# A graph-attention layer on one core: the last 512 adjacency columns of the last quarter summed densely, and the tail of the program put in another order

## The chip, the cores and the metric

One core of a Trainium2 chip. The metric is the device time of one execution in microseconds (us); of several executions the median counts. All arrays start and end in HBM.

## The reference

The input is x, 4096 nodes of 128 features in float32, and a 4096x4096 adjacency of zeros and ones, denser towards low row and column numbers (an entry is 1 with a probability that falls as one over the root of both numbers). What is computed, cut short:

```python
h = relu(layernorm(x))
Wh = h @ W0
e = leaky_relu((Wh @ a[:128])[:, None] + (Wh @ a[128:])[None, :], 0.2)
e = where((adj > 0) | eye(N), e, -9e15)
x = x + softmax(e, axis=1) @ Wh
h = relu(layernorm(x))
weights = where(adj < 1.0, exp(-(1/adj - 1)**2 / 0.5), 0.0)
return x + weights @ (h @ W1 + B)
```

For an adjacency of zeros and ones the last sum is zero, so the program checks that no entry is anything else and would take a general path (not run here) if one were.

## The kernel before, in words

The 64 MB of the adjacency are read once, as 32 chunks of 2 MB (128 partitions x 4096 numbers) through a ring of six buffers, `adj_ring`. `chunk(i)` (line 58) says what chunk i holds: quarter s of the rows (1024 rows each), column block c (1024 columns), and half h (512 of the quarter's rows). Two chunks with the same s and c make a step; there are four steps to a quarter, sixteen in all. In the last quarter the column blocks come in the order 3, 0, 1, 2 (steps 12 to 15, chunks 24 to 31).

Each chunk is read by three engines.

- TensorE packs it (`pack`, L613 to L645): for every 512 columns one matmul writes a code of the column (L629), and four matmuls per half chunk add the entries times powers of two (L642), so that after both halves of a step a PSUM bank holds, per partition and column, one word with the bits of eight rows.
- VectorE or ScalarE checks that its entries are zeros and ones: VectorE for 13 chunks in one SCALAR_TENSOR_TENSOR (L1134), 26 and 28 among them, ScalarE for 19 in two passes (L952, L961), 24, 25, 27, 29, 30 and 31 among them.
- A buffer is given back when it is packed and checked; SyncE then issues the load of the chunk six later (L394 to L405).

From the words the edges are found. VectorE takes the eight largest words of each stretch of columns (`scan`, L1162, MAX8 into `cand`), then picks the best per partition over the steps of a piece (`pick`, L1175; `PIECES`, line 75, says which steps make a piece: steps 0 to 3, 4 to 7, 8 to 11, 12 to 14, and 15 alone). What a partition picks beyond its own slots goes into slots that a set of partitions shares (`place` on TensorE, L683; `pick_shared`, L1208; `place_shared`, L710). `decode` (L1295) and `decode_shared` (L1252) turn words into a column number and row bits. GpSimd then fetches a row of `node_table` (130 numbers of a node: its weight factor and scaled features) per slot by indirect DMA (L544), in groups g of eight such gathers or fewer. VectorE makes edge weights and spreads them (`weigh`, L1321), and TensorE adds them to eight accumulator tiles by matmuls (`scatter`, L773, sixteen matmul records for eight tiles). The last group, g = 9, has four gathers, each weighed and added by itself (`weigh_last`, L1380; `scatter_last`, L790). Group 6 (eight gathers) and 7 (eight shared gathers) belong to the third quarter, group 8 to steps 12 to 14, group 9 to step 15.

Beside this run dense parts for the first 128 columns (`column`, L1422; `add_columns`, L740) and for each node's edge to itself (`own_weights`, L979, on ScalarE; `add_own`, L758). When all groups of a quarter are added, `epilogue(s)` (L1445) divides and adds x; the last quarter's is split in three (`finish_last`, L1462), each with its own store.

There is no scheduler: each engine runs its instructions in the order of the code. The tables of lines 122 to 145 say behind which chunk i of its main loop an engine does what (SCAN_AT, PICK_AT, DECODE_AT, WEIGH_AT, CHECK_LATE, EPILOGUE_AT on VectorE, SCATTER_AT, PLACE_BEHIND, ADD_COLUMNS_AT and ADD_OWN_AT on TensorE), and lines 602 to 616 (VectorE) and 849 to 859 (TensorE) are the tail behind the loop. Engines wait for one another by semaphores.

## Time and profile before

| what | value |
|---|---|
| median of 3 runs | 216.37 us (216.04 to 217.75) |
| the profiled execution | 217.44 us |
| its span, first to last instruction | 215.6 us |
| busy in the span: TensorE, VectorE, ScalarE, GpSimd | 72%, 84%, 88%, 62% |
| read from HBM | 74.06 MB |

The span is the stretch that the profile covers; the execution's own time has 1.84 us more around it. The profiled execution is slower than the median by 1.07 us, so that differences are worked out inside the profile and laid on the median. In the rows below, times are us from the span's start.

### The profile page before, as it was taken

How to read it: one execution, taken by the hardware profiler on the slowest of the kernel's cores; microseconds unless marked ns; L12 is line 12 of the kernel's file. 1: busy time of each engine (PE TensorE's matmuls, PEld its weight loads, DVE VectorE, ACT ScalarE, POOL GpSimd, SP SyncE). 2: the span in 40 equal slices, each digit the busy share in tenths (PEclk: the TensorE clock that was granted, in tenths of full speed). 3: DMA queues.
4: the chain of work that ended last, by engine and by line, in shares of the span. 5: the costliest groups of instructions: out<-in, count | busy, mean ns of one | idle time of the engine just before them, and what ended most of it. 6: DMA issues, size and time to landing. Idle time of an engine off the chain costs nothing.

```text
span 215.6 us, 3229 instructions
## 1 busy us (share of the span) xinstructions
PE 154.3 (72%) x956; PEld 103.7 (48%) x970; DVE 182.0 (84%) x535; ACT 189.3 (88%) x207; POOL 132.8 (62%) x140
## 2 busy tenths in 40 slices
PE   0186779983794992989929997499392977799472
PEld 0074565440362760549615844186341654668361
DVE  7993999999979999999488796995986499878855
ACT  0699987599899999999999999799999994999960
POOL 3980002295000588888878888888787788667450
PEclk9999999996599698599985999999979799999995
DMA  5999999999999999999999999999999999961303
GB/s 166 355 413 410 410 408 408 409 411 405 418 418 409 409 393 405 391 400 393 402 388 387 394 401 394 404 387 400 394 387 389 386 401 393 406 229 43 115 23 103
DMA packets 22259, 76.81 MB, mean 356 GB/s; under 512 B 2527, under 2 KB 3126, under 8 KB 22240
## 3 DMA queue, kind: packets, MB, share of 16 engines
q1 hardware_dynamic: 18912, 71.31, 84.7%
q0 software_dynamic: 2912, 5.22, 7.0%
q8 instruction: 8, 0.13, 0.2%
q10 hardware_dynamic: 416, 0.07, 0.2%
q14 instruction: 11, 0.09, 0.1%
HBM read 74.06 MB, written 4.23 MB: 363 GB/s over the span
## 4 chain that ended last, share of the span: by engine, by line
DMA 36%; DVE 31%; PE 18%; issue 7%; ACT 5%; SPq 1%; POOL 1%; POOLq 0%; DVEq 0%
DMA adj_ring<-in_adj 35%; DVE summed L1134 10%; PE bank L642 9%; DVE cand L1172 3%; ACT spread L921 3%; DVE hub_w L1415 3%; PE bank L769 2%; DVE x_sb L1458 2%; PE bank L754 2%; PE bank L761 2%; SPq L383 1%; DMA gathered_rows<-node_table,shared_index 1%; DVE stats L1114 1%; PE bank L629 1%; DVE shared_slots L1230 1%
## 5 line engine op out<-in xcount | busy, mean ns | idle before, releaser
L544 POOL DMA_INDIRECT gathered_rows<-node_table,index x48 | 76.0, 1584 | 36.5 <-DVE index L1309 22.5
L952 ACT ACTIVATE trash_a<-adj_ring,below_one 128x4096 fp8e4<-128x4096 f32 x19 | 70.4, 3705 | 5.7 <-DMA adj_ring<-in_adj 5.2
L642 PE MATMUL bank<-adj_ring,pack_w 128*128 128x512 bf16 (+3 forms) x255 | 70.0, 402 | 2.4 <-DMA adj_ring<-in_adj 1.5
L961 ACT ACTIVATE trash_a<-adj_ring 128x4096 fp8e4<-128x4096 f32 x19 | 68.7, 3614 | 0.5
L1134 DVE SCALAR_TENSOR_TENSOR summed<-adj_ring 128x4096 fp8e4<-128x4096 f32 x13 | 58.0, 4458 | 4.3 <-DMA adj_ring<-in_adj 4.2
L642 PEld LDWEIGHTS bank<-adj_ring,pack_w 128*128 128x128 bf16 x262 | 26.1, 104 | 31.5 <-issue 8.8
L544 POOL DMA_INDIRECT gathered_rows<-node_table,shared_index x24 | 33.2, 1382 | 9.6 <-issue 6.7
L1172 DVE MAX8 cand<-bank 128x8 f32<-128x120 f32 (+25 forms) x82 | 23.3, 351 | 3.9 <-PE bank L642 3.9
L769 PE MATMUL bank<-gathered_rows,spread 128*128 128x129 f32 x160 | 20.9, 282 | 3.9 <-DVE spread L1398 2.4
L769 PEld LDWEIGHTS bank<-gathered_rows,spread 128*128 128x128 f32 x160 | 19.4, 194 | 5.1 <-issue 4.8
L629 PE MATMUL bank<-codes,code_w 128*128 128x512 bf16 x25 | 11.2, 448 | 8.5 <-DMA adj_ring<-in_adj 5.6
L678 PE MATMUL bank<-whe,hub_w 128*128 128x129 f32 x64 | 10.4, 316 | 5.1 <-DVE hub_w L1419 5.0
L921 ACT ACTIVATE spread<-x_sb,shift,rstd 128x128 f32<-128x128 f32 x32 | 13.2, 497 | 0.3 <-DVE shift L1126 0.3
L678 PEld LDWEIGHTS bank<-whe,hub_w 128*128 128x128 f32 x64 | 9.1, 219 | 7.0 <-DVE hub_w L1419 6.8
L491 POOL PARTITION_ALL_REDUCE ends_all<-ends x1 | 1.4, 1442 | 17.3 <-DVE ends L1539 17.3
L565 PE MATMUL bank<-ident,spread 128*128 128x128 f32 x32 | 6.3, 327 | 7.8 <-ACT spread L921 7.8
L577 PE MATMUL bank<-w_sb,gathered_rows 128*128 128x130 f32 x64 | 9.8, 300 | 1.4 <-ACT whe L935 1.3
L1442 DVE SCALAR_TENSOR_TENSOR col_w<-r_rows,hub_whe,bank 128x512 f32<-128x512 f32 (+1 forms) x6 | 4.2, 708 | 7.4 <-PE bank L609 7.4
L629 PEld LDWEIGHTS bank<-codes,code_w 128*128 128x128 bf16 x32 | 3.7, 115 | 13.7 <-DMA adj_ring<-in_adj 6.2
L577 PEld LDWEIGHTS bank<-w_sb,gathered_rows 128*128 128x128 f32 x64 | 8.6, 208 | 2.7 <-ACT gathered_rows L927 2.4
L985 ACT ACTIVATE own_w<-ident,w_self 128x128 f32<-128x128 f32 x32 | 9.7, 386 | 0.0
L699 PE MATMUL bank<-slots,own_lane 128*32 128x16 f32 (+1 forms) x24 | 1.4, 188 | 10.5 <-issue 10.5
(190 smaller groups left out, 258.4 us busy)
## 6 DMA issues: line engine op xcount, KB each, us to landing
adj_ring<-in_adj SPq DMA_DIRECT2D x32, 2048.0 KB, 23.6
node_table<-gathered_rows POOLq DMA_DIRECT2D x4, 520.0 KB, 8.3
x_sb<-in_x SPq DMA_DIRECT2D x8, 256.0 KB, 5.9
out<-x_sb SPq DMA_DIRECT2D x3, 512.0 KB, 14.2
gathered_rows<-node_table,index POOLq DMA_INDIRECT x48, 5.9
gathered_rows<-node_table,shared_index POOLq DMA_INDIRECT x24, 5.4
out<-x_sb SPq DMA_DIRECT2D x2, 192.0 KB, 2.1
out<-x_sb SPq DMA_DIRECT2D x1, 128.0 KB, 1.9
```

The costliest lines, as they stand in the source:

```text
L544: pool.indirect_dma_start(out=rows[:, g % RING_GROUPS * GE + t, :], out_offset=None, in_=table, in_offset=bass.IndirectOffsetOnAxis(ap=row ...
L577: last = nc.tensor.matmul(bank[6 + half][:, b * (D + 2):(b + 1) * (D + 2)], hT[:, nb * P:(nb + 1) * P], w0_sb[:, :], start=(b == 0), stop= ...
L629: nc.tensor.matmul(to[:, :], code_w[:, 2 * c + half, :], codes[:, :], start=True, stop=False, skip_group_check=True)
L642: last = nc.tensor.matmul(to[:, lo:hi], pack_w[:, k, :], ring_hi[:, i % AR, row_at + lo:row_at + hi], start=False, stop=(k == KB - 1), ski ...
L678: last = nc.tensor.matmul(bank[7][:, 0:E1], hub_w[:, m % 2, b, :], whe[:, 4 * HUB_ORDER[m] + b, ONE:ONE + E1], start=(m + b == 0), stop=(m ...
L769: return nc.tensor.matmul(acc_of(SUPER_OF_GROUP[g], t), spread[:, g % 2, at * KB:(at + 1) * KB, :], rows[:, g % RING_GROUPS * GE + turn, G ...
L921: last = nc.scalar.activation(hn_block(b), x_sb[:, b, :], ACT.Identity, bias=shift[:, b:b + 1], scale=rstd[:, b:b + 1])
L952: nc.scalar.activation(trash_a[:, :], ring[:, i % AR, :], ACT.Sign, bias=below_one[:, :], scale=-1.0, accum_out=signs[:, n:n + 1], saturat ...
L961: nc.scalar.activation(trash_a[:, :], ring[:, i % AR, :], ACT.Abs, accum_out=sizes[:, n:n + 1], saturate=False).then_inc(checked_a, 1)
L985: last = nc.scalar.activation(own_w[:, t, :], ident[:, :], ACT.Copy, scale=w_self[:, nb:nb + 1])
L1134: nc.vector.scalar_tensor_tensor(trash_v, ring[:, i % AR, :], 1.0, ring[:, i % AR, :], ALU.is_ge, ALU.not_equal, accum_out=bad_v[:, n:n + ...
L1172: last = nc.vector.max(cand[:, at * 8:(at + 1) * 8], word_bank(step, half)[:, lo:hi])
```

## The change

The last chunk of the adjacency is no longer a half of step 15. `kernel()` on the host lays the last quarter's columns 2048 to 3071 out anew, without arithmetic, as an input `adj_tail` of two times 2 MB beside the old one. Its first half holds columns 2048 to 2559 for all 1024 rows in the packing's layout. This is chunk 28, the narrow one; it makes step 14 alone, in one PSUM bank. Step 15 is column block 1, whose halves are chunks 29 and 30. The second half of `adj_tail`, chunk 31, holds columns 2560 to 3071 turned, so that partitions are columns, in four blocks of 128 columns, each with its own DMA and semaphore. These are not packed and scanned: VectorE multiplies each block with the weights max(row factor, column factor) (`weigh_dense`, one SCALAR_TENSOR_TENSOR of 128x1024), and TensorE adds it to the eight accumulator tiles (`add_dense`). The 512 rows of the node table for that are loaded by SyncE ahead of chunk 20 into `summed`, in which the checks of VectorE wrote until chunk 11; from chunk 14 on they write over `hub_mask`.

The third quarter's shared slots get sets of eight partitions rather than four (`PIECES`), so that its group 7 has four gathers in place of eight; for that a second table of row factors (`r_oct2`) is made near the start. The tables that order the loop are changed from chunk 25 on, and the tail behind the loop is written anew.

```diff
+NARROW, DENSE = 28, CHUNKS - 1
+DENSE_AT = 5 * BW
+DB = 4
 def chunk(i):
+    if i >= NARROW:
+        return SG - 1, 1 if i in (29, 30) else 2, int(i > 29)
...
-PIECES = [((0, 1, 2, 3), 32, 16, 32, 4), ((4, 5, 6, 7), 24, 16, 16, 4), ((8, 9, 10, 11), 24, 8, 32, 4),
+PIECES = [((0, 1, 2, 3), 32, 16, 32, 4), ((4, 5, 6, 7), 24, 16, 16, 4), ((8, 9, 10, 11), 24, 8, 32, 8),
...
-CHECK_LATE = {22: 22, 27: 26, 29: 28}
+CHECK_LATE = {22: 22, 26: 26, 30: 28}
...
-ADD_COLUMNS_AT = {13: 0, 21: 1, 28: 2}
-EPILOGUE_AT = {20: 0, 28: 1}
...
+ADD_COLUMNS_AT = {13: 0, 21: 1, 27: 2}
+EPILOGUE_AT = {20: 0, 27: 1, 31: 2}
...
+                if i == NARROW:
+                    sp.dma_start(ring[:, i % AR, :].rearrange("p (a n) -> p a n", a=HK),
+                                 adj_tail[0].rearrange("a p n -> p a n")).then_inc(adj_ready[i % AR], 16)
+                    return
+                if i == DENSE:
+                    for b in range(DB):
+                        sp.dma_start(dense_adj[:, b, :], adj_tail[1, b]).then_inc(dense_ready[b], 16)
+                    return
...
+                if i == 20:
+                    sp.wait_ge(table_stored, 16 * SG)
+                    sp.wait_ge(checked_v, DVE_CHECKED.index(14))
+                    sp.dma_start(dense_whe, table[DENSE_AT:DENSE_AT + BW, :].rearrange("(p b) c -> p b c", b=DB)).then_inc(
+                        dense_whe_loaded, 16)
...
+            def add_dense(b):
+                pe.wait_ge(dense_set, b + 1)
+                pe.wait_ge(dense_whe_loaded, 16)
+                for t in range(KB):
+                    nc.tensor.matmul(acc_of(SG - 1, t), dense_w[:, b, t, :], dense_whe[:, b, GQ:GQ + E1], start=False,
+                                     stop=True, skip_group_check=True)
...
+            def weigh_dense(b):
+                dve.wait_ge(dense_ready[b], 16)
...
+                nc.vector.scalar_tensor_tensor(dense_w[:, b, :, :].rearrange("p t m -> p (t m)"),
+                                               r_rows[:, :, :].rearrange("p t m -> p (t m)"), dense_whe[:, b, AQ:AQ + 1],
+                                               dense_adj[:, b, :], ALU.max, ALU.mult).then_inc(dense_set, 1)
...
-            weigh(7)
             scan(STEPS - 1)
             pick(4)
-            epilogue(2)
+            weigh_dense(0)
             pick_shared(4)
+            weigh_dense(1)
             decode_shared(4)
+            weigh_dense(2)
             weigh(8)
+            weigh_dense(3)
             weigh_last(0)
```

The first place is VectorE around the check of chunk 26 (the SCALAR_TENSOR_TENSOR of 128x4096), at the start of the last quarter. `cand<-bank2` are the scans of step 13, `edge_w` begins `weigh(6)`, `rden` begins `epilogue(1)`. Before:

```order
L1372 TENSOR_TENSOR spread<-same,hq_of_e 128x512
L1442 SCALAR_TENSOR_TENSOR col_w<-r_rows,hub_whe,bank7 128x8x64 [waits col_turned,col_added,r_rows_set]
L1134 SCALAR_TENSOR_TENSOR summed,bad<-adj_ring 128x4096 [waits checked_v,adj_ready2]
L1442 SCALAR_TENSOR_TENSOR col_w<-r_rows,hub_whe,bank7 128x8x64 [waits col_turned]
L1172 MAX cand<-bank2 128x8 [waits packed]
...
L1348 TENSOR_TENSOR edge_w<-r_slots,gathered_rows 128x64 [waits spread_set,gathered2,bits_set]
...
L1453 RECIPROCAL rden<-bank4 128x3 [waits acc_read,scattered]
...
L1134 SCALAR_TENSOR_TENSOR summed,bad<-adj_ring 128x4096 [waits checked_v,adj_ready4]
L1172 MAX cand<-bank0 128x8 [waits packed]
```

Now; L1204 is the check, L1543 the column weights, L1554 the epilogue:

```order
L1473 TENSOR_TENSOR spread<-same,hq_of_e 128x512
L1204 SCALAR_TENSOR_TENSOR hub_mask,bad<-adj_ring 128x4096 [waits checked_v,adj_ready2]
L1543 SCALAR_TENSOR_TENSOR col_w<-r_rows,hub_whe,bank7 128x8x64 [waits col_turned,col_added,r_rows_set]
L1554 RECIPROCAL rden<-bank4 128x3 [waits acc_read,scattered]
...
L1440 TENSOR_TENSOR edge_w<-r_slots,gathered_rows 128x64 [waits spread_set,gathered2,bits_set]
...
L1543 SCALAR_TENSOR_TENSOR col_w<-r_rows,hub_whe,bank7 128x8x64 [waits col_turned]
L1242 MAX cand<-bank2 128x8 [waits packed]
...
L1440 TENSOR_TENSOR same<-r_oct2,gathered_rows 128x256 [waits spread_set,gathered3,shared_on_set]
...
L1242 MAX cand<-bank0 128x8 [waits packed]
```

The check of chunk 26 now stands ahead of both column weights, and the epilogue ahead of `weigh(6)`; `weigh(7)` (`same<-r_oct2`), which came behind step 14 and its decoding, now stands ahead of step 14's scan (`cand<-bank0`), with the check of chunk 28 behind that.

The second place is the tail of VectorE: `pick_shared(4)` begins with `placed<-bank7`, `decode_shared(4)` with `shared_i<-bank7` and gives `shared_index`, for which GpSimd waits with group 9. Before:

```order
L1185 TENSOR_REDUCE fullest<-cand 128x1 [waits placed_set,full_seen,merged,scanned]
...
L1453 RECIPROCAL rden<-bank4 128x3 [waits acc_read,scattered]
...
L1458 SCALAR_TENSOR_TENSOR x_sb<-bank4,rden,x_sb 128x128 [waits epilogue_step]
...
L1221 TENSOR_TENSOR placed<-bank7,iota 16x64 [waits shared_placed_set,shared_seen,shared_picked,merged]
...
L1266 CAST shared_i<-bank7 128x4 [waits shared_on_set,shared_index_set,shared_done]
...
L1278 TENSOR_TENSOR shared_index<-shared_column,shared_empty 128x4 [waits weight_step,gathered1,shared_step]
...
L1348 TENSOR_TENSOR edge_w<-r_slots,gathered_rows 128x64 [waits spread_set,gathered0,bits_set]
...
L1387 SCALAR_TENSOR_TENSOR same<-r_oct,gathered_rows,shared_on 128x64 [waits spread_set,shared_on_set,last_gathered0]
```

Now; L1403 is `weigh_dense`:

```order
L1554 RECIPROCAL rden<-bank4 128x3 [waits acc_read,scattered]
...
L1242 MAX cand<-bank2 128x8 [waits picked,packed]
...
L1255 TENSOR_REDUCE fullest<-cand 128x1 [waits placed_set,full_seen,merged,scanned]
...
L1403 SCALAR_TENSOR_TENSOR adj_ring<-r_rows,summed,adj_ring 128x1024 [waits col_turned,packed,checked_v,dense_whe_loaded,dense_ready0]
L1296 TENSOR_TENSOR placed<-bank7,iota 16x64 [waits shared_placed_set,shared_seen,shared_picked,merged]
...
L1403 SCALAR_TENSOR_TENSOR adj_ring<-r_rows,summed,adj_ring 128x1024 [waits dense_ready1]
L1341 CAST shared_i<-bank7 128x4 [waits shared_on_set,shared_index_set,shared_done]
...
L1353 TENSOR_TENSOR shared_index<-shared_column,shared_empty 128x4 [waits weight_step,gathered1,shared_step]
...
L1403 SCALAR_TENSOR_TENSOR adj_ring<-r_rows,summed,adj_ring 128x1024 [waits dense_ready2]
L1440 TENSOR_TENSOR edge_w<-r_slots,gathered_rows 128x64 [waits spread_set,gathered0,bits_set]
...
L1403 SCALAR_TENSOR_TENSOR adj_ring<-r_rows,summed,adj_ring 128x1024 [waits dense_ready3]
L1488 SCALAR_TENSOR_TENSOR same<-r_oct,gathered_rows,shared_on 128x64 [waits spread_set,shared_on_set,last_gathered0]
```

`epilogue(2)` (`rden<-bank4`) has gone from behind the last pick to ahead of the last scan (`cand<-bank2`), and four `weigh_dense` stand in the tail, two of them ahead of `shared_index`.

The third place is the tail of TensorE, from the last shared words on. Before (L761 is `add_own`, L769 the scatter):

```order
L719 MATMUL bank7<-turn_of_tq,stats 128x4 [waits shared_placed_set]
L761 MATMUL bank0<-whe,own_w 128x129 [waits own_w_set]
L761 MATMUL bank0<-whe,own_w 128x129 x2
...
L769 MATMUL bank0<-gathered_rows,spread 128x129 [waits spread_set,gathered0]
...
L769 MATMUL bank0<-gathered_rows,spread 128x129 [waits part_spread,last_gathered0]
...
L769 MATMUL bank0<-gathered_rows,spread 128x129 [waits part_spread,last_gathered1]
```

Now (L797 is `add_dense`, L831 the scatter):

```order
L797 MATMUL bank0<-summed,adj_ring 128x129 [waits dense_whe_loaded,dense_set]
...
L777 MATMUL bank7<-turn_of_tq,stats 128x4 [waits shared_placed_set]
L797 MATMUL bank0<-summed,adj_ring 128x129 [waits dense_whe_loaded,dense_set]
...
L797 MATMUL bank0<-summed,adj_ring 128x129 [waits dense_whe_loaded,dense_set]
...
L831 MATMUL bank0<-gathered_rows,spread 128x129 [waits spread_set,gathered0]
...
L797 MATMUL bank0<-summed,adj_ring 128x129 [waits dense_whe_loaded,dense_set]
...
L831 MATMUL bank0<-gathered_rows,spread 128x129 [waits part_spread,last_gathered0]
...
L831 MATMUL bank0<-gathered_rows,spread 128x129 [waits part_spread,last_gathered1]
```

`add_own` has gone ahead of this place, and four times eight dense products of float32 stand around the last words and the last whole group, one of them between that group and the four parts of the last one.

## Rows read from the trace of the kernel before

**Rows 1.** The page's slices of the span, 40 equal ones: DMA busy in tenths.
```profile
DMA  5999999999999999999999999999999999961303
```
**Rows 2.** Timeline of TensorE: start us, us, line, operation, operands, count, idle time before and releaser.
```profile
165.46 0.39 PE L629 MATMUL bank<-codes,code_w 128*128 128x512 bf16 x1 [4.03 <-DMA adj_ring<-in_adj]
...
177.00 0.39 PE L629 MATMUL bank<-codes,code_w 128*128 128x512 bf16 x1 [1.35 <-DMA adj_ring<-in_adj]
...
204.94 2.47 PE L769 MATMUL bank<-gathered_rows,spread 128*128 128x129 f32 x20 [1.20 <-DVE spread L1359]
...
209.50 0.68 PE L769 MATMUL bank<-gathered_rows,spread 128*128 128x129 f32 x4 [0.68 <-DVE spread L1398]
211.21 1.20 PE L769 MATMUL bank<-gathered_rows,spread 128*128 128x129 f32 x4 [1.03 <-DVE spread L1398]
```
**Rows 3.** Timeline of VectorE, the last quarter up to the last scan.
```profile
169.84 0.75 DVE L1442 SCALAR_TENSOR_TENSOR col_w<-r_rows,hub_whe,bank 128x512 f32<-128x512 f32 x1 [4.35 <-PE bank L609]
170.51 4.42 DVE L1134 SCALAR_TENSOR_TENSOR summed<-adj_ring 128x4096 fp8e4<-128x4096 f32 x1
...
178.42 0.30 DVE L1453 RECIPROCAL rden<-bank 128x3 f32<-128x3 f32 x3
...
180.70 4.42 DVE L1134 SCALAR_TENSOR_TENSOR summed<-adj_ring 128x4096 fp8e4<-128x4096 f32 x1
...
185.04 1.49 DVE L1172 MAX8 cand<-bank 128x8 f32<-128x24 f32 x5
...
190.98 0.43 DVE L1348 TENSOR_TENSOR same<-r_quad,gathered_rows 128x256 f32<-128x256 f32 x1 [0.41 <-DMA gathered_rows<-node_table,shared_index]
...
194.59 1.43 DVE L1172 MAX8 cand<-bank 128x8 f32<-128x272 f32 x4 [1.47 <-PE bank L642]
```
**Rows 4.** Timeline of VectorE, the tail behind the last pick.
```profile
196.48 0.30 DVE L1453 RECIPROCAL rden<-bank 128x3 f32<-128x3 f32 x3
...
198.76 0.20 DVE L1221 TENSOR_TENSOR placed<-bank,iota 16x64 f32<-16x64 f32 x1
...
201.79 0.16 DVE L1266 CAST shared_i<-bank 128x4 int32<-128x4 f32 x1 [0.41 <-PE bank L719]
...
202.19 0.16 DVE L1278 TENSOR_TENSOR shared_index<-shared_column,shared_empty 128x4 int32<-128x4 int32 x1
...
203.05 0.22 DVE L1348 TENSOR_TENSOR edge_w<-r_slots,gathered_rows 128x64 f32<-128x64 f32 x1
...
203.56 1.22 DVE L1359 TENSOR_TENSOR spread<-edge_w,lane_of_p 128x1024 f32<-128x1024 f32 x1
...
209.27 0.17 DVE L1468 RECIPROCAL rden<-bank 128x3 f32<-128x3 f32 x1
...
210.26 0.28 DVE L1387 SCALAR_TENSOR_TENSOR same<-r_oct,gathered_rows,shared_on 128x64 f32<-128x64 f32 x1
...
212.66 0.61 DVE L1472 SCALAR_TENSOR_TENSOR x_sb<-bank,rden,x_sb 128x128 f32<-128x128 f32 x2
```
**Rows 5.** Timeline of GpSimd: gathers of groups 6 and 7.
```profile
166.08 1.00 POOL L544 DMA_INDIRECT gathered_rows<-node_table,index  x1 [0.30 <-issue]
167.38 1.00 POOL L544 DMA_INDIRECT gathered_rows<-node_table,shared_index  x1 [0.30 <-issue]
...
171.29 4.50 POOL L544 DMA_INDIRECT gathered_rows<-node_table,shared_index  x1 [0.30 <-issue]
...
180.98 5.01 POOL L544 DMA_INDIRECT gathered_rows<-node_table,shared_index  x1 [0.30 <-issue]
```
**Rows 6.** The page's DMA issues: operands, engine, count, median us from issue to landing.
```profile
gathered_rows<-node_table,shared_index POOLq DMA_INDIRECT x24, 5.4
```
**Rows 7.** Stretches: us; busy us of PE, PEld, DVE, ACT, POOL; TensorE clock granted; DMA share; GB/s.
```profile
111.50:118.20 6.70, 5.69 (x29) 3.44 (x30) 5.88 (x22) 6.67 (x7) 5.18 (x6) 0.50 1.03 385
...
166.10:169.40 3.30, 3.30 (x10) 1.23 (x9) 0.00 (x0) 3.27 (x3) 2.69 (x3) 0.50 1.03 394
...
210.50:213.50 3.00, 1.43 (x6) 1.01 (x6) 2.37 (x12) 0.00 (x0) 0.00 (x0) 0.50 0.36 130
```

More of the change, by code:

```diff
@@ L106, in piece_segments @@
     s = SUPER_OF_PIECE[n]
-    columns = {chunk(2 * step)[1] for step in PIECES[n][0]}
-    return [x for x in SEGMENTS[s] if x[0] // 2 in columns]
+    banks = {b for step in PIECES[n][0] for b in banks_of(step)}
+    return [x for x in SEGMENTS[s] if x[0] in banks]
 NCAND = max(len(piece_segments(n)) for n in range(len(PIECES))) * 8
@@ L611, in turn_columns, with pack_narrow @@
                 last.then_inc(col_turned, 1)
+            def pack_narrow():
+                pe.wait_ge(adj_ready[NARROW % AR], (NARROW // AR + 1) * 16)
+                step = step_of(NARROW)
+                to = word_bank(step, 0)
+                pe.wait_ge(scanned, scanned_by(step - 2) - 1)
+                nc.tensor.matmul(to[:, :], code_w[:, banks_of(step)[0], :], codes[:, :], start=True, stop=False,
+                                 skip_group_check=True)
+                for k in range(KB):
+                    last = nc.tensor.matmul(to[:, :], pack_w[:, k, :], ring_hi[:, NARROW % AR, k * BW:(k + 1) * BW],
+                                            start=False, stop=(k == KB - 1), skip_group_check=True)
+                last.then_inc(packed, 1)
             def pack(i):
+                if i == NARROW:
+                    return pack_narrow()
                 s, c, h = chunk(i)
-                step = i // 2
+                step = step_of(i)
                 pe.wait_ge(adj_ready[i % AR], (i // AR + 1) * 16)
@@ L816, in _ @@
             lane_scores()
-            for i in range(CHUNKS):
+            for i in range(DENSE):
                 pack(i)
@@ L948, in check @@
                 n = ACT_CHECKED.index(i)
-                act.wait_ge(adj_ready[i % AR], (i // AR + 1) * 16)
+                if i == DENSE:
+                    for b in range(DB):
+                        act.wait_ge(dense_ready[b], 16)
+                else:
+                    act.wait_ge(adj_ready[i % AR], (i // AR + 1) * 16)
                 if n >= 1:
```

208 lines of the change are left out of this document (130 added, 78 removed).

## The prediction

> **What bounds the kernel now.** I read the page's slices first: the DMA engines are nine tenths busy or more from the second slice through the 35th [rows 1], so the chunks arrive as fast as they can until the slice that begins at 188.7 us, and then there is a tail of some 23 us in which little is loaded. Next the timelines, to see what that tail consists of. TensorE waits for chunk 26 at 165.46 and for chunk 28 at 177.00 [rows 2], that is 5.8 us a chunk; the last scan starts at 194.59, released by TensorE's packing of chunk 31 [rows 3]. From there one chain runs to the end: last scan and pick, `epilogue(2)`, the shared pick (198.76), the shared decoding with `shared_index` at 202.19, the last gathers, their weights, and the last division, which ends at 212.66 + 0.61 = 213.27 [rows 4]. The stores make the rest of the 215.6 us.
>
> But VectorE, not chunk 31, sets the pace before that. From the column weights at 169.84 on it has short waits only, 0.41 for a gather and 1.47 for the last packing [rows 3], and before that one long one, 4.35, for the first columns of the quarter. The reader should keep three things apart: VectorE's own work, the gathers that it waits for, and the last chunk. The change shortens what depends on the last chunk and adds work to VectorE and TensorE.
>
> **Up to group 7: what the moved check fills, and what it holds up.** The load of 512 table rows ahead of chunk 20 (128 x 520 numbers, 266 KB) goes through the saturated SyncE queue. At the 394 GB/s of a late stretch [rows 7] that is 0.7 us on every later chunk. Its bounds are 0, if the four removed gathers give that time back, and 0.7; I take 0.6 and have chunk 26 at 166.1. The check of chunk 26, 4.42 us [rows 3], now runs there at once, to 170.5, in the hole of 4.35 us. Taken alone that gains all of it.
>
> The hole was covered by nothing on VectorE, but GpSimd was gathering in it. The gather that began at 171.29, 0.78 us into the check of 170.51, took 4.50 us instead of 1.00 and ended at 175.79, which is 0.86 behind the check's end at 174.93; the one at 180.98 did the same beside the check of 180.70 [rows 3, 5]. So a check costs GpSimd one gather of its own length. Now it meets the last gather of group 6, which began at 166.08 [rows 5]: this ends at 170.5 + 0.9 = 171.4. The four gathers of group 7 follow at GpSimd's pitch of 1.3 (166.08 to 167.38), at 171.7, 173.0, 174.3 and 175.6, and the last lands 5.4 later [rows 6], at 181.0. VectorE gets there earlier: column weights to 171.3, `epilogue(1)` 2.28 (178.42 to 180.70) to 173.6, group 6 landing at 166.08 + 5.4 + 4.4 = 175.9, its weights 1.73 (as 203.05 to 204.78 [rows 4]), columns 0.75 and a scan of 1.49 to 179.9. `weigh(7)` thus waits for 1.1 us and starts at 181.0. From issue to landing a gather is bounded below by its issue, 1.00, and above by 6.0: the one held from 180.98 to 185.99 was what VectorE waited for until 190.98, 10.0 later, 4.0 of them its hold. I take the median of the page, which is near the upper end.
>
> At this place the trace and a rule part. The Trainium skill (SBUF — State Buffer, Who interferes with whom) infers that a VectorE operation with two SBUF inputs takes only the read side of the port that it shares with GpSimd, and that writing descriptors needs the other side, so that such an operation would not hold up a gather. The gather of 4.50 us beside a two-input check says that it does here. By the rule the stall would go; what that gives is the first rival.
>
> **From group 7 to the last index.** `weigh(7)` takes 2.14 (190.98 to 194.59 - 1.47 = 193.12 [rows 3]), to 183.1. From the scan of step 14 to the end of the shared pick of piece 3 was 185.04 to 190.98 - 0.41 = 190.57, 5.53 us; the narrow step has two maxima in place of five, 3/5 of 1.49 less: 4.6, to 187.7. The check of chunk 28 takes 4.34 (180.70 to 185.04), to 192.1; `epilogue(2)` 2.28 (196.48 to 198.76 [rows 4]), to 194.4. The last scan and pick take 1.89 (194.59 to 196.48), to 196.3. So VectorE is done here at 196.3 with what in before it had done at 198.76: 2.5 us ahead. TensorE has chunk 30 packed by then: at 5.8 us a chunk it lands by 189.2, and TensorE's work behind the merge of the third piece (chunk 29, group 7, six column tiles, chunk 30) is some 7 us from 185.8, to 193.
>
> `weigh_dense` has no row. Nearest are the same operation on 512 elements, 0.75, and on 4096, 4.42 [rows 3]; between them lie 1.02 ns an element, so 1024 take 1.27, of which about 0.07 overlaps with the next, as with the columns (0.75 against a start to start of 0.67, 169.84 to 170.51). I take 1.2; the bounds stay 0.75 and 4.42. Two of them stand ahead of the index: 196.3 + 1.2 = 197.5; the shared pick 2.62 (198.76 to 201.79 - 0.41 = 201.38), 200.1; the second, 201.3; decoding to the index 0.56 (201.79 to 202.19 + 0.16), 201.9 against 202.35. Of the 2.5 us ahead, 2.4 are two dense blocks less 0.4 of waiting that they cover: 0.45 remain. Chunk 31, at the same 5.8 us a chunk, is there by 195, before its first block is used, and is no longer waited for.
>
> **The end.** Decoding ends 1.26 behind its start, at 202.6; the third block 203.8; `weigh(8)` 1.73, 205.5; the fourth block 206.7. On TensorE 16 matmuls of float32 take 2.47 - 0.68 = 1.79 us (20 against 4 [rows 2]). From 203.8 it has the third block, group 8, the fourth block and two parts of the last group: 16 + 16 + 16 + 8 matmuls, 6.3 us with nothing between, 210.2 with 0.1 to start. TensorE, which waited here in before, now ends last. The last gathers, 0.45 earlier and perhaps 0.9 later for a `weigh_dense` beside them, land by 210.3 and are covered. Then as in before: the first division 0.99 (209.27 to 210.26), 211.2; the last weights 0.95 (210.26 to 211.21), 212.15; four matmuls 0.68 at full clock in place of 1.20, 212.85; last division 0.86 (212.41 to 213.27), 213.7. That is 0.4 later than 213.27. The profiled execution of 217.44 would be 217.9, and on the median 216.37 + 0.4 = **216.8 us**. A measurement tells about 1% (2.2 us) from no change, so this is no change.
>
> The other edits I cost at nothing. The second `r_oct` table and its matmul fall near the start, where the chunks come as fast as the DMA engines allow; without that cover they are under 1 us. Four blocks and a narrow chunk are the same bytes in the same rows of 4 KB. `own_weights(3)` now runs while ScalarE waits for chunk 29, so ScalarE ends some 2 us earlier, but nobody waits for it.
>
> **Rivals.** (1) The gathers are not held up. Then group 7 lands at 171.29 + 5.4 = 176.7, before VectorE comes to it (171.3 + 2.28 + 1.73 + 0.75 + 1.49 = 177.5), and all behind it moves up by 181.0 - 177.5 = 3.5, TensorE's packing of chunk 28 (177.6, 2.0 us) just allowing it: 216.8 - 3.5 = **213.3, faster**. This is what the skill's rule on the shared port would make of it. Against it are both held gathers of rows 5; for it, that 166.08 and 166.1 are a tie: should that one gather pass ahead, 1.3 us are won (215.5, still no change). (2) TensorE's clock falls in the dense blocks. It was at its lower level, 1.2 GHz, from 166.1 to 169.4 behind 4.03 us without work, for 6.7 us from 111.5, and from 210.5 on, where the same four matmuls took 1.20 in place of 0.68 [rows 2, 7]. The blocks come with gaps between them from 196 on. If it falls at the place where TensorE ends last, after 203.8, a stretch of 3.3 to 6.7 us does half the work and costs 1.7 to 3.3: 218.5 to 220.1, **219.3, slower**. It decides only there; earlier, VectorE covers it. Against it: between 203.8 and 210 TensorE would have no gap at all. (3) The change does not do what it says, because group 8 is gathered late: its eight gathers start near 187, the check of chunk 28 holds one for 4 us, and GpSimd may come to the last group only at 202.4. That is 0.5 us, 217.3, inside no change.
>
> **How the numbers follow.** Forecast, with (3) and the tie: 0.59. Rival (1) and other ways in which waits vanish: 0.24. Rival (2) and dense weights nearer their upper bound (each 1 us more on three of them is 3 us): 0.17. So faster by over 1% 0.24, within 1% 0.59, slower 0.17. The forecast's own range is 215.3 (0.75 a block, three of them on the path, -1.4) to 218.4 (gather latency, +1, and a short fall of the clock). For 8 in 10 it must reach into both rivals: 213.0 to 219.6.
>
> **What would show it.** Right: a check of 4.4 us from about 166, one gather beside it that ends 0.9 behind it, `weigh(7)` waiting for a gather at about 181, `weigh_dense` at 1.2, TensorE without a gap from 204 to 210, the last division ending near 213.7. Wrong: `weigh(7)` before 179, or TensorE's clock at half behind 200, or a scan of step 15 that waits for TensorE.

## The result, and the profile after

The changed kernel takes 219.17 us in the median (219.11 to 219.82) where the kernel before takes 216.53 beside it (216.04 to 217.75): a ratio of 1.0123, 95% interval 1.0091 to 1.0155. It is slower by a little more than 1%. It lies inside the range of 213.0 to 219.6, near its upper end, and above the forecast's own 215.3 to 218.4: the forecast of 216.8 and of "no change" was 2.4 us too low. A second set of runs of the same kernel gave 220.14 (218.98 to 220.60), ratio 1.0152 (1.0114 to 1.0191). Ratios are of undisturbed runs of the same set, without those over 1.5% above a kernel's fastest (below: two of ten without dense work, its profiled one among them, five of ten without dense work but with filler, five of twelve with the orders combined), so they can differ from the quotient of two medians.

The profiled execution took 219.82 us, span 218.0, last division at 215.12 + 0.61 = 215.73 (213.27 before, forecast 213.7). VectorE's timeline, the last quarter up to the last scan, which answers to [rows 3]:

```profile
166.24 4.41 DVE L1204 SCALAR_TENSOR_TENSOR hub_mask<-adj_ring 128x4096 fp8e4<-128x4096 f32 x1
...
176.03 0.23 DVE L1440 TENSOR_TENSOR edge_w<-r_slots,gathered_rows 128x64 f32<-128x64 f32 x1 [2.43 <-issue]
...
181.30 0.42 DVE L1440 TENSOR_TENSOR same<-r_oct,gathered_rows 128x256 f32<-128x256 f32 x1 [1.59 <-issue]
...
186.40 0.17 DVE L1377 CAST words_i<-bank 128x8 int32<-128x8 f32 x1 [0.79 <-PE bank L764]
...
188.33 4.43 DVE L1204 SCALAR_TENSOR_TENSOR hub_mask<-adj_ring 128x4096 fp8e4<-128x4096 f32 x1
...
195.69 1.49 DVE L1242 MAX8 cand<-bank 128x8 f32<-128x24 f32 x5 [0.64 <-PE bank L700]
```

The check of chunk 26 stands where it was forecast, and the two waits for gathers are there, 2.43 and 1.59 (forecast 2.3 and 1.1). The profile names no releaser for them; each ends 4.5 to 4.6 us behind the end of the last gather that the group needs (171.52 and 176.72 on GpSimd), and from 164 us on a gather of this run takes 2.5 to 5.5 us from issue to landing. New is the last line: the last scan waits 0.64 us for TensorE's packing of chunk 30, and ahead of the decoding at 186.40 VectorE waited 0.79 for TensorE, where before it was 0.55 for the same step. The reason stands in TensorE's timeline, beside [rows 2]:

```profile
165.88 0.39 PE L687 MATMUL bank<-codes,code_w 128*128 128x512 bf16 x1 [1.83 <-DMA adj_ring<-in_adj]
...
185.26 0.57 PE L757 MATMUL bank<-slots,own_oct 128*16 128x8 f32 x16 [3.89 <-issue]
...
186.59 1.92 PE L700 MATMUL bank<-adj_ring,pack_w 128*128 128x512 bf16 x4
...
193.69 1.97 PE L700 MATMUL bank<-adj_ring,pack_w 128*128 128x512 bf16 x8
...
211.12 1.50 PE L831 MATMUL bank<-gathered_rows,spread 128*128 128x129 f32 x12
214.16 0.68 PE L831 MATMUL bank<-gathered_rows,spread 128*128 128x129 f32 x4 [1.54 <-DVE spread L1499]
```

TensorE stood 3.89 us ahead of the placing of piece 3 (L757). The four packing matmuls at 186.59 then take 1.92 us; in the run with filler below, at full clock, four take 1.06. Two stretches give the granted clock as the last but two figure (columns as in [rows 7]):

```profile
185.26:189.50 4.24, 4.10 (x25) 2.06 (x27) 3.25 (x14) 4.21 (x4) 1.58 (x2) 0.50 1.03 414
203.00:212.50 9.50, 8.90 (x76) 8.64 (x76) 7.71 (x26) 3.55 (x3) 4.17 (x4) 1.00 0.08 16
```

So TensorE's clock was at its lower level (1.2 GHz) from 185.3 to 189.5, and at the full one (2.4 GHz) behind 203, where the second rival had looked for its fall. The tail on VectorE, beside [rows 4]:

```profile
198.08 1.28 DVE L1403 SCALAR_TENSOR_TENSOR adj_ring<-r_rows,summed,adj_ring 128x1024 f32<-128x1024 f32 x1 [0.34 <-issue]
...
203.41 0.17 DVE L1353 TENSOR_TENSOR shared_index<-shared_column,shared_empty 128x4 int32<-128x4 int32 x1
...
208.37 0.32 DVE L1488 SCALAR_TENSOR_TENSOR same<-r_oct,gathered_rows,shared_on 128x64 f32<-128x64 f32 x1
...
212.21 0.18 DVE L1569 RECIPROCAL rden<-bank 128x3 f32<-128x3 f32 x1 [1.55 <-PE bank L831]
...
213.22 0.27 DVE L1488 SCALAR_TENSOR_TENSOR same<-r_oct,gathered_rows,shared_on 128x64 f32<-128x64 f32 x1
...
215.12 0.61 DVE L1573 SCALAR_TENSOR_TENSOR x_sb<-bank,rden,x_sb 128x128 f32<-128x128 f32 x2
```

A dense block takes 1.28 us (1.20 from start to start). No weighing of group 8 or 9 waits for a gather any more: `weigh(8)` at 205.53 and `weigh_last(0)` at 208.37 follow their predecessors. VectorE works without a pause from 198.08 to 210.66 and then waits 1.55 us for TensorE. The index is 1.2 later than before (203.58 against 202.35 at its end), and from there to the last division's end it is 12.15 us against 10.92.

GpSimd, beside [rows 5]: the gather that met the check ends 0.87 us behind it (166.24 + 4.41 = 170.65), and the four of group 7 follow. Later the check of chunk 28 holds the second gather of group 8 in the same way (4.65 us from 189.00).

```profile
166.89 4.63 POOL L588 DMA_INDIRECT gathered_rows<-node_table,index  x1 [0.30 <-issue]
171.82 1.00 POOL L588 DMA_INDIRECT gathered_rows<-node_table,shared_index  x1 [0.30 <-issue]
```

### The profile page after: what moved, and what is told of

The parts are those of the page before. It is cut to its first block, busy times and chain, and to the rows that moved or that the text cites. A ratio compares the mean times of both kernels' runs of the same rounds, so it can differ in the third digit from the quotient of the medians.

```text
span 218.0 us, 3371 instructions
## 1 busy us (share of the span) xinstructions
PE 160.5 (74%) x1021; PEld 111.0 (51%) x1035; DVE 186.8 (86%) x539; ACT 190.0 (87%) x209; POOL 124.2 (57%) x136
## 4 chain that ended last, share of the span: by engine, by line
DVE 30%; PE 26%; DMA 22%; issue 10%; ACT 9%; SPq 1%; DVEq 0%
DMA adj_ring<-in_adj 22%; PE bank L700 8%; DVE summed L1204 8%; PE bank L831 4%; DVE hub_w L1516 3%; DVE cand L1242 3%; ACT spread L987 3%; PE bank L814 3%; PE bank L822 2%; PE bank L797 2%; ACT trash_a L1022 2%; ACT trash_a L1031 2%; PE bank L687 1%; DVE adj_ring L1403 1%; SPq L447 1%
## 5 line engine op out<-in xcount | busy, mean ns | idle before, releaser
L588 POOL DMA_INDIRECT gathered_rows<-node_table,index x48 | 76.8, 1599 | 44.3 <-DVE index L1384 30.8
L700 PE MATMUL bank<-adj_ring,pack_w 128*128 128x512 bf16 (+3 forms) x239 | 67.5, 409 | 3.7 <-DMA adj_ring<-in_adj 2.5
L700 PEld LDWEIGHTS bank<-adj_ring,pack_w 128*128 128x128 bf16 x246 | 25.1, 106 | 31.5 <-issue 10.1
L1204 DVE SCALAR_TENSOR_TENSOR summed<-adj_ring 128x4096 fp8e4<-128x4096 f32 x7 | 31.5, 4500 | 0.1
L1204 DVE SCALAR_TENSOR_TENSOR hub_mask<-adj_ring 128x4096 fp8e4<-128x4096 f32 x6 | 26.5, 4419 | 4.8 <-DMA adj_ring<-in_adj 4.8
L588 POOL DMA_INDIRECT gathered_rows<-node_table,shared_index x20 | 23.8, 1192 | 8.6 <-issue 5.8
L1242 DVE MAX8 cand<-bank 128x8 f32<-128x120 f32 (+25 forms) x80 | 22.7, 350 | 3.1 <-PE bank L700 3.1
L831 PE MATMUL bank<-gathered_rows,spread 128*128 128x129 f32 x160 | 20.0, 277 | 1.5 <-DVE spread L1499 1.5
L831 PEld LDWEIGHTS bank<-gathered_rows,spread 128*128 128x128 f32 x160 | 19.3, 193 | 2.2 <-issue 2.0
L797 PE MATMUL bank<-summed,adj_ring 128*128 128x129 f32 x64 | 8.1, 280 | 1.5 <-DVE adj_ring L1403 1.5
L1516 DVE TENSOR_SCALAR hub_w<-r_hub,whe 128x128 f32<-128x128 f32 x32 | 8.9, 354 | 0.0
```

The lines of the kernel that those rows point to most:

```text
L588: pool.indirect_dma_start(out=rows[:, g % RING_GROUPS * GE + t, :], out_offset=None, in_=table, in_offset=bass.IndirectOffsetOnAxis(ap=row ...
L700: last = nc.tensor.matmul(to[:, lo:hi], pack_w[:, k, :], ring_hi[:, i % AR, row_at + lo:row_at + hi], start=False, stop=(k == KB - 1), ski ...
L831: return nc.tensor.matmul(acc_of(SUPER_OF_GROUP[g], t), spread[:, g % 2, at * KB:(at + 1) * KB, :], rows[:, g % RING_GROUPS * GE + turn, G ...
L1204: nc.vector.scalar_tensor_tensor(trash_v[int(i >= 14)], ring[:, i % AR, :], 1.0, ring[:, i % AR, :], ALU.is_ge, ALU.not_equal, accum_out=b ...
L1242: last = nc.vector.max(cand[:, at * 8:(at + 1) * 8], word_bank(step, half)[:, lo:hi])
L1516: last = nc.vector.tensor_scalar(hub_w[:, m % 2, b, :], r_hub[:, :], whe[:, nb, QA:QA + 1], whe[:, nb, AA:AA + 1], ALU.mult, ALU.max)
```

## The experiments

Whole times of one kernel differ by 1.6 us and more from run to run, and the check of chunk 26 begins anywhere from 165.6 to 167.0 with the loads. What a step does is therefore also read in the profiled execution, as the stretch from the start of that check to the start of the last division, called the late stretch here. It is one execution of each kernel, and the two of the changed kernel differ by 0.64 us, so smaller differences can be chance.

| run | ratio to before (95%) | late stretch, us |
|---|---|---|
| changed kernel | 1.0123 (1.0091 to 1.0155) | 48.88 |
| the same again | 1.0152 (1.0114 to 1.0191) | 48.24 |
| chunk 29 packed first | 1.0116 (1.0074 to 1.0158) | 47.95 |
| filler ahead of the placing | 1.0119 (1.0079 to 1.0158) | 47.90 |
| no dense sums | 1.0131 (1.0078 to 1.0183) | 49.43 |
| no dense work | 1.0020 (0.9987 to 1.0054) | 46.87 |
| no dense work, with filler | 0.9945 (0.9899 to 0.9991) | 43.61 |
| end reordered | 1.0063 (1.0027 to 1.0099) | 48.13 |
| check of chunk 26 late | 1.0122 (1.0083 to 1.0161) | (moved) |
| orders combined | 0.9961 (0.9925 to 0.9997) | 45.48 |
| and group 6 behind the scan | 0.9906 (0.9875 to 0.9937) | 43.82 |

**TensorE's pause, by order and by filler.** The first:

```
-PLACE_BEHIND = {15: 1, 23: 2, 28: 3}
+PLACE_AT = {8: 0, 29: 3}
+PLACE_BEHIND = {15: 1, 23: 2}
```

> Only the order on TensorE differs from the changed kernel: chunk 29 is packed ahead of the placing of piece 3 instead of behind it. Theory A (the 3.89 us in which TensorE stood before that placing left it at half clock, and the packings of chunks 29 and 30 came late for VectorE's last scan): the first packing matmuls of chunk 29 start near 182.7 us and take 1.07 us each four instead of 1.92, the placing starts where it did, the decode comes 0.2 us sooner, chunk 30 is packed by about 192 us, the last scan follows the epilogue without its 0.64 us wait, and the whole comes out near 218.3 us (0.9 us less than 219.2). Rival B (VectorE covers it, what it gains at the scan it waits again later, for TensorE's dense sums): 219.0 to 219.3 us. In both the last third from the last index to the end stays at 12.1 us.

The second leaves the order alone and adds, ahead of that `place(3)`:

```
+if i == 28:
+    pe.wait_ge(col_w_set, 2 * SG)
+    for _ in range(12):
+        nc.tensor.matmul(bank[7][:, :], pack_w[:, 0, :], ring_hi[:, NARROW % AR, 0:BW], start=True,
+                         stop=True, skip_group_check=True)
```

> The changed kernel's order is kept; twelve packing matmuls of 512 columns whose sums nobody reads are added on TensorE in the 3.89 us in which it stood before the placing of piece 3 (some 2.7 us of work, so about 1.2 us of standing are left). They take no work away, so only the clock can give something back. Theory A (it is the half clock after the pause): the placing's 16 matmuls take 0.3 instead of 0.57 us, the packing of chunk 29 goes at 1.07 us for four, chunk 30 is packed by about 193.3 us instead of 195.7, the last scan does not wait, and the time is near 218.3 us. Rival B (it is the order, chunk 29 behind the placing, and not the clock): the granted clock may rise, but the last scan still waits for TensorE, and the time is within 0.2 us of 219.2.

TensorE's timeline in the run with filler:

```profile
181.45 2.88 PE L910 MATMUL bank<-adj_ring,pack_w 128*128 128x512 bf16 x12
185.48 0.55 PE L757 MATMUL bank<-slots,own_oct 128*16 128x8 f32 x16 [1.16 <-issue]
...
186.42 1.06 PE L700 MATMUL bank<-adj_ring,pack_w 128*128 128x512 bf16 x4
...
191.56 1.97 PE L700 MATMUL bank<-adj_ring,pack_w 128*128 128x512 bf16 x8
```

Its clock in the stretch behind the placing, 1.00 in place of 0.50:

```profile
185.20:189.50 4.30, 4.02 (x38) 2.84 (x39) 3.51 (x15) 4.27 (x4) 1.59 (x2) 1.00 1.02 413
```

VectorE's decoding and its last scan there:

```profile
186.38 0.17 DVE L1382 CAST words_i<-bank 128x8 int32<-128x8 f32 x1 [0.55 <-PE bank L764]
...
194.95 1.48 DVE L1247 MAX8 cand<-bank 128x8 f32<-128x24 f32 x5
```

Added work made TensorE faster: four packing matmuls take 1.06 again, the decoding waits 0.55 instead of 0.79, the last scan not at all, and the late stretch is 0.98 shorter; with the order changed it is 0.93. So the half clock is what delays TensorE, since no order differs here: from the placing to the end of chunk 30's packing it takes 8.05 us (185.48 to 193.53) in place of 10.40 (185.26 to 195.66). The whole time did not follow: both ratios are that of the first set. That is why the changed kernel was run again.

> The changed kernel itself, unaltered, beside the others of this row, because the runs with the placing moved and with filler were shorter by 0.9 us from the check of chunk 26 to the last division (47.9 against 48.9 us) and yet not in their whole time. If the load-bound part ahead of that check varies from run to run and with the place where a kernel runs, this kernel comes out at or above its first 219.2 us here (219.2 to 220.3), with the stretch from that check to the last division again 48.8 to 49.0 us. If instead the 0.9 us are paid back before the check by those two kernels themselves, it is again at 219.2 and its check again begins at 166.2 us where theirs began at 166.5 and 167.0.

The first of the two expectations held for the whole time, 220.14, 0.6 to 0.8 above the two others, though on another chip (the kernel before took 216.59 beside it and 216.44 beside them). It did not hold for the late stretch, 48.24, beside which the filler's is only 0.34 shorter. TensorE's timeline:

```profile
185.70 0.55 PE L757 MATMUL bank<-slots,own_oct 128*16 128x8 f32 x16 [3.90 <-issue]
...
189.15 1.22 PE L700 MATMUL bank<-adj_ring,pack_w 128*128 128x512 bf16 x3
```

VectorE in the same execution:

```profile
195.39 1.48 DVE L1242 MAX8 cand<-bank 128x8 f32<-128x24 f32 x5
```

Again a pause of 3.90 and half clock behind it, but three matmuls from 189.15 take 1.22, and the granted clock is 1.00 from 189.6 on, where in the first execution it is still 0.50 up to 190.5; the packing of chunk 30 just makes it, and the last scan does not wait. Six profiles have this pause, of 3.79 to 4.17 us. In them the last scan waited 0, 0, 0.64, 0.65, 0.77 and 0.77 us for TensorE, and the decoding 0.77 to 0.79 in five and 0.55 in one. The clock costs up to 0.24 at the placing and 0 to 0.8 at the scan. A gain of 0.6 to 0.8 in the whole time is within the intervals, so the ratios do not show it: that the clock delays the last scan is shown, that repairing it shortens the whole is not.

**What the dense columns cost.** All four `weigh_dense` and all four `add_dense` calls are taken out in the first run, the `add_dense` calls alone in the second, so both results lack those columns.

> Leaves out the last 512 columns' work: the four weighings of the dense blocks on VectorE and the four sums on TensorE. Their loads stay. Theory: two weighings (2.5 us) stand before the last index, so it comes at about 201.0 instead of 203.58 us, and behind it nothing of the two other weighings and of TensorE's 64 matmuls is left; the end is then set by the last gathers, issued from 201.9 us on and landed near 208.9, so weigh and scatter of the last part end near 210.2 and the last division near 211.3: about 214.8 us in all, 4.4 less. Rival (the dense work lies beside the gathers, as the weighing of group 8 did in the kernel before): 217.5 us or more.

> Leaves out the four dense sums on TensorE (64 matmuls), keeps the four weighings on VectorE. Theory (TensorE ends last from the third dense sum on): the last index stays at 203.6 us, the first division starts behind the third part's weighing at about 210.7 instead of 212.21 us, without a wait for TensorE, and the whole is near 217.7 us, 1.5 less. Rival (VectorE ends last, TensorE only seems late): within 0.3 us of 219.2. With the run without any dense work this splits the price into VectorE's part and TensorE's.

Both fell short. Without the sums nothing was won at all. TensorE's scatters of that run:

```profile
207.16 5.40 PE L831 MATMUL bank<-gathered_rows,spread 128*128 128x129 f32 x28 [4.91 <-DVE spread L1447]
```

The granted clock in its pause, and in those scatters:

```profile
203.00:207.00 4.00, 0.00 (x0) 0.00 (x0) 3.90 (x12) 3.05 (x3) 2.29 (x3) 0.50 0.04 7
207.10:211.00 3.90, 3.84 (x18) 3.88 (x19) 3.21 (x10) 0.00 (x0) 1.78 (x2) 0.50 0.15 27
```

Without the dense sums TensorE stands 4.91 us, the clock is at 0.50, and 28 scatter matmuls take 5.40 us. The first division came at 212.15, as with all the sums. The dense sums cost the end nothing on balance: they keep the clock up for what follows. The run without any dense work shows the same (28 matmuls 5.89), and waits for gathers came back in it, 0.69, 1.52 and 0.53 us (in the kernel before 0.81, 0.76 and 0.56). So a filler was put into that pause as well:

```
...
 place_shared(4)
+pe.wait_ge(scanned, scanned_by(STEPS - 1))
+for _ in range(12):
+    nc.tensor.matmul(bank[3][:, :], pack_w[:, 0, :], ring_hi[:, 30 % AR, 0:BW], start=True,
+                     stop=True, skip_group_check=True)
```

> Leaves out the four dense weighings and the four dense sums, as before, and puts twelve packing matmuls of 512 columns whose sums nobody reads (2.7 us) into the 4.1 us in which TensorE then stood between the placing of the shared slots and the scatter of group 8. Theory (without the dense sums TensorE's clock falls, and that hides what they cost): the 28 scatter matmuls, 5.89 us at half clock in the run without filler, take about 3.3 us again, the first division no longer waits 1.01 us for TensorE, and the stretch from the check of chunk 26 to the last division falls from 46.9 to about 45.9 us, 3.0 below the changed kernel's. Rival (the gathers' landing alone sets that end): the clock rises but the stretch stays at 46.7 to 46.9 us.

TensorE's scatters in the run without filler, and the pause ahead of them:

```profile
205.20 5.89 PE L831 MATMUL bank<-gathered_rows,spread 128*128 128x129 f32 x28 [4.11 <-DVE spread L1447]
```

The filler and the scatters here:

```profile
198.90 4.75 PE L918 MATMUL bank<-adj_ring,pack_w 128*128 128x512 bf16 x11 [0.34 <-issue]
203.48 3.33 PE L831 MATMUL bank<-gathered_rows,spread 128*128 128x129 f32 x28
```

GpSimd around the check of chunk 26 in that run:

```profile
165.00 0.99 POOL L588 DMA_INDIRECT gathered_rows<-node_table,index  x1 [0.30 <-issue]
166.30 4.66 POOL L588 DMA_INDIRECT gathered_rows<-node_table,shared_index  x1 [0.31 <-issue]
```

VectorE there, that check and the weighing of group 6:

```profile
165.66 4.43 DVE L1204 SCALAR_TENSOR_TENSOR hub_mask<-adj_ring 128x4096 fp8e4<-128x4096 f32 x1
...
174.11 0.21 DVE L1440 TENSOR_TENSOR edge_w<-r_slots,gathered_rows 128x64 f32<-128x64 f32 x1
```

The 28 matmuls take 3.33, and ahead of the first division VectorE waits 0.38 instead of 1.01. The late stretch, 43.61, is 2.3 below the 45.9 expected, for two reasons. In this execution the last gather of group 6 passed ahead of the check (165.00 to 165.99; the check holds the next one, of group 7). The weighing of group 6 starts 8.45 us behind the check's start, not 9.73 to 9.91 as in the eight other profiles with this order, and the weighing of group 7 comes 1.26 sooner. And the last group's gathers were waited for 0.57 us in all instead of 2.05 (group 8's for 1.03 instead of 0.69). Against the first filler run the dense work thus costs 47.90 - 43.61 - 1.26 = 3.0 us in these two executions, with TensorE at full clock in what they scatter at the end, or 1.9 with the gather waits of the run without filler (1.1 more, an estimate). Where its absence also halves the clock it is 1.4 to 2.0 (48.24 and 48.88 less 46.87); but the execution of 46.87 lies 0.9 us above its kernel's median, and by the ratios, 1.0020 against 1.0123 and 1.0152, it is 2.2 to 2.9. No run fixes this price more closely than 1.4 to 3.0 us. The ratio of 0.9945 is no proof of the filler either: the median of all ten executions is 216.94 beside 216.59.

**The end.** VectorE's tail behind the loop stands in lines 1602 to 1616 of the kernel before (not 602 to 616).

```
-def add_dense(b):
+def add_dense(b, tiles=range(KB)):
...
-add_dense(3)
+add_dense(3, range(4))
 scatter_last(0)
 scatter_last(1)
+add_dense(3, range(4, KB))
...
+weigh_last(3)
 finish_last(0)
-weigh_last(3)
```

> All work is kept; two orders at the end differ: on VectorE the last part of group 9 is weighed ahead of the first division instead of behind it, and on TensorE the last dense sum's tiles 4 to 7 come behind the first two last scatters. Theory (VectorE's 1.55 us wait for TensorE at the first division, and TensorE's 1.54 us wait for the last weighing, are one and the same knot): the first division starts about 1 us sooner after the third part's weighing, TensorE has no wait for the last part, and the last division ends 1.0 us sooner: 47.9 instead of 48.9 us from the check of chunk 26. Rival (TensorE's 64 dense matmuls set the end in any order): less than 0.3 us.

VectorE's end in that run:

```profile
208.29 0.32 DVE L1489 SCALAR_TENSOR_TENSOR same<-r_oct,gathered_rows,shared_on 128x64 f32<-128x64 f32 x1
...
211.74 0.17 DVE L1570 RECIPROCAL rden<-bank 128x3 f32<-128x3 f32 x1
...
213.92 0.61 DVE L1574 SCALAR_TENSOR_TENSOR x_sb<-bank,rden,x_sb 128x128 f32<-128x128 f32 x2
```

From `weigh_last(0)` to the last division it is 5.63 instead of 6.75 (6.68 to 6.75 in the five profiles with the old end and all its work): 1.1 less, and TensorE's wait for the last part is gone. The late stretch fell by 0.75 only: with TensorE's clock at 0.50 until 191.0 in this execution, the last scan came 29.83 us behind the check of chunk 26, not 29.45. The ratio is 1.0063.

**The check of chunk 26.**

```
-CHECK_LATE = {22: 22, 26: 26, 30: 28}
+CHECK_LATE = {22: 22, 27: 26, 30: 28}
```

> Only the place of the check of chunk 26 differs from the changed kernel: it stands on VectorE behind the weighing of group 6 instead of ahead of the turned columns of chunk 26, the hole that it filled is empty again. Theory (what the check wins in the hole it loses again because the last gather of group 6 and all of group 7's stand behind it on GpSimd): the last gather of group 6 takes 1.0 instead of 4.63 us, the weighing of group 6 starts near 172.8 without the wait of 2.43, the check runs about 174.6 to 179, the weighing of group 7 starts near 181 with little or no wait, and the scan of chunk 28 near 183.0 where the changed kernel has 183.4: 0 to 0.5 us less in all, so a ratio of 1.010 to 1.015 to the kernel before. Rival (the filled hole is a clear gain, the gathers would be late anyway): the scan of chunk 28 comes 2 to 4 us later, a ratio of 1.022 or more.

The last gather of group 6 on GpSimd:

```profile
168.00 1.00 POOL L588 DMA_INDIRECT gathered_rows<-node_table,index  x1 [0.31 <-issue]
```

VectorE from group 6 to the scan of chunk 28:

```profile
173.73 0.23 DVE L1440 TENSOR_TENSOR edge_w<-r_slots,gathered_rows 128x64 f32<-128x64 f32 x1 [1.20 <-issue]
...
175.39 4.42 DVE L1204 SCALAR_TENSOR_TENSOR hub_mask<-adj_ring 128x4096 fp8e4<-128x4096 f32 x1
...
181.66 0.41 DVE L1440 TENSOR_TENSOR same<-r_oct,gathered_rows 128x256 f32<-128x256 f32 x1
...
183.77 0.75 DVE L1242 MAX8 cand<-bank 128x8 f32<-128x272 f32 x2
```

No gather of groups 6 and 7 is held. Group 6's weighing waits 1.20 (none was expected), group 7's waits for nothing, and from the weighing of group 5 (165.41; 164.30 in the changed kernel) to the scan at 183.77 it is 18.36 us against 19.13. The ratio is that of the changed kernel. Filling the hole of 4.35 us won nothing that these runs can tell, because the check keeps GpSimd from issuing.

**What the rows point to.** The check of chunk 28 goes ahead of `weigh(7)`, chunk 29 and group 7's scatter ahead of the placing, the columns' sum behind chunk 30, and the end as above:

```
-CHECK_LATE = {22: 22, 26: 26, 30: 28}
+CHECK_LATE = {22: 22, 26: 26}
+CHECK_AMID = {28: 28}
-PLACE_BEHIND = {15: 1, 23: 2, 28: 3}
+PLACE_BEHIND = {15: 1, 23: 2, 29: 3}
...
+                if i in CHECK_AMID:
+                    check(CHECK_AMID[i])
                 if i in WEIGH_AT:
...
```

> All work is kept. Four orders differ from the changed kernel: the check of chunk 28 stands on VectorE ahead of the weighing of group 7, where VectorE waited 1.59 us, instead of behind the decode of piece 3; on TensorE chunk 29's packing and the scatter of group 7 go ahead of the placing of piece 3; the sum of the hub's columns goes behind the packing of chunk 30; and the end is ordered as in the run on the tail. Theory (from check 26 on, VectorE's work in a row sets the time, with waits of 2.43, 1.59, 0.79, 0.64 and 1.55 us in it): the waits of 1.59, most of 0.79, 0.64 and most of 1.55 go, the last scan starts about 27.1 us after the check of chunk 26 instead of 29.45, and the last division ends about 45.5 us after it instead of 48.9: 215.8 us where the changed kernel has 219.2, 0.3% below the kernel before. Rival (what is moved up waits for chunks: chunk 30 lands near 187.7 us, so the last scan can't start before 190.5): 217.5 us or more.

The late stretch is 45.48, as expected, though not every wait went: ahead of the decoding it is 0.91, where 0.79 had been. The ratio is 0.9961 (0.9925 to 0.9997), but the median of all twelve executions is 216.83 beside 216.59, so a gain over the kernel before is not clear. One more order, `weigh(6)` moved from i = 27 to directly ahead of `check(28)`:

> All work is kept. On top of the run that combined the orders, the weighing of group 6 stands behind the turned columns of chunk 27 and the scan of step 13 instead of ahead of them, since VectorE waited 2.54 us for that group's gathers and both were ready. Theory (VectorE's row of work from check 26 on sets the time): the wait of 2.54 us shrinks to about 0.4, the check of chunk 28 then starts near 177.9 instead of 179.4, the weighing of group 7 follows it without a wait at about 182.3, and the last division starts 1.5 to 2.0 us sooner than there: 43.5 to 44.0 us from the check of chunk 26 instead of 45.5, a ratio near 0.988 to the kernel before. Rival (the loads bind: chunk 28 lands at 177.2, chunk 30 at 187.7, and the packings stand behind them): 45 us or more from that check, ratio 0.994 or more.

VectorE from the scan of step 13 to the last scan:

```profile
174.41 1.35 DVE L1244 MAX8 cand<-bank 128x8 f32<-128x144 f32 x5
175.79 0.23 DVE L1442 TENSOR_TENSOR edge_w<-r_slots,gathered_rows 128x64 f32<-128x64 f32 x1
...
177.45 4.42 DVE L1206 SCALAR_TENSOR_TENSOR hub_mask<-adj_ring 128x4096 fp8e4<-128x4096 f32 x1
...
181.79 0.42 DVE L1442 TENSOR_TENSOR same<-r_oct,gathered_rows 128x256 f32<-128x256 f32 x1
...
191.72 1.48 DVE L1244 MAX8 cand<-bank 128x8 f32<-128x24 f32 x5
```

No wait for a gather is left between 170 and 182, the late stretch is 43.82, and the kernel takes 214.57 us (214.34 to 215.53) where the one before takes 217.15 (215.61 to 217.45): a ratio of 0.9906 (0.9875 to 0.9937). Ahead of the decoding VectorE now waits 1.41, behind the scatter of group 7 on TensorE. It is the change with its work in another order, and faster than both kernels. Whether such orders would do as much for the kernel before, without dense columns, no run shows.

## Why the prediction was right and wrong

Right, by its own list of what would show it (all but the last division near 213.7): the check at 166.24 (166.1), the held gather 0.87 behind it (0.9), `weigh(7)` at 181.30 (181.0), 1.20 a dense block (1.2), group 8's gathers all out by 201.53 and so not in the way, as against the third rival, TensorE without a gap from 205.65 until its wait for the last weights. That the filled hole is paid back on GpSimd is shown by the late check. The tie in the first rival is shown too: where one gather passed ahead, the weighings came 1.3 us sooner, as it said. The Trainium skill (SBUF — State Buffer, Who interferes with whom) infers that a two-input VectorE operation does not hold up descriptor writing; here every gather that met such a check ended 0.86 to 0.91 us behind it, so for these gathers the measurement decides against that. Whether it is their descriptors that wait or the reading of their `index`, no run tells apart.

The step that failed is in "From group 7 to the last index": "TensorE has chunk 30 packed by then ... some 7 us from 185.8, to 193". It priced that work at full clock. The work took from 185.26 to 195.66, 10.40 us, and 8.05 in the run with filler, because the 3.89 us without work ahead of it, which the new order makes by leaving nothing for TensorE between group 6 and the placing, put the clock at its lower level. The second rival had the mechanism but not the place: "It decides only there; earlier, VectorE covers it". VectorE does not cover it: in four of the six profiles with this pause the scan of step 15 waits for TensorE, which the prediction had named as a sign that it was wrong. That the rival's 219.3 lies beside the measured 219.17, and that the range reached so far up on its account, is luck: the fall came at another place and cost 0.88 us in the rows, not 1.7 to 3.3.

How the 2.0 us at the last division add up (215.73 less 213.7): `weigh(7)` 0.30 late. Up to the check of chunk 28, 188.33 for 187.7, another 0.33, of which 0.24 is the placing at half clock. The last scan 195.69 for 194.4, 0.64 of it the wait. From it to the first dense block 2.39 for 1.89: scan and pick themselves were 0.16 longer (five maxima for four), and VectorE stood 0.34 ahead of the first block, which waits for several semaphores. Which of them came last isn't settled; it is 0.34 in all nine profiles with this block, so hardly work that ends at changing times. From the index to the end 12.15 for 11.8. The filler run takes back these 0.24 and 0.64, 0.88 of the 2.0, in the rows. The rest of the 2.4 us in the median is that the changed kernel's profiled execution lay 0.65 above its median where that of before lay 1.07 above.

The term for the end was right in its mechanism, TensorE last, but took the order as given: reordered, 1.1 us of it go with all matmuls kept. And the terms for the dense work did not say that TensorE's sums have a second effect: they hold the clock.

Why slower than before, then: 1.2 us at the index, where two dense blocks and the waits at half clock use up what the shorter last chunk had won, and 1.2 behind it, where VectorE's two further blocks cover the gathers that before it had to wait for, and end in the knot with TensorE.

## What to carry to other kernels

When an edit leaves TensorE standing, as here for 3.79 to 4.91 us, price what comes behind the pause at the lower clock too, and look for who waits for it. A few matmuls that nobody reads can hold the clock, but shorten the whole only if somebody waits; here the gain was not clear of the noise, and real work moved into the pause did the same. When a long VectorE operation with two inputs in memory, like this check, is moved into a hole, look at what GpSimd issues in that stretch, and move it to where the gathers are out. When one engine works nearly without a pause, list its remaining waits in order of size and ask of each what is ready behind it: here orders alone turned 1.2% slower into 0.9% faster.

## What was not expected of the hardware

Less work on TensorE was not less time: 28 scatter matmuls took 5.40 to 5.89 us behind 4 to 5 us without work, and 3.33 with filler in between, though the filler itself ran at the lower level (eleven recorded matmuls in 4.75 us). How long the lower level lasted behind a pause of 3.8 to 4.2 us differed from one execution to the next, and the last scan waited 0 to 0.77 us with it.

It is not the check alone that holds a gather. In the kernel before, the first operation below ran on VectorE to 178.50, and the gather, 1.00 us otherwise, ended 0.88 behind it:

```profile
177.28 1.22 DVE L1359 TENSOR_TENSOR spread<-edge_w,lane_of_p 128x1024 f32<-128x1024 f32 x1
...
177.41 1.97 POOL L544 DMA_INDIRECT gathered_rows<-node_table,shared_index  x1 [0.30 <-issue]
```

GpSimd's ordinary operations are held as well, not only its gathers. With the check of chunk 28 at 179.42 (to 183.83) in the run that combined the orders, this one, 0.30 us in the changed kernel, ended 0.16 us behind it:

```profile
179.62 4.37 POOL L573 TENSOR_SCALAR bad<-sd_sum 128x16 f32<-128x16 f32 x1
```
